# Moving the marks of two wide pairs from VectorE to GpSimd in a two-block sequence model

## What is computed

```python
dots = jnp.einsum('bhid,bhjd->bhij', q, k) * QK_SCALE
dots = jnp.einsum('hg,bgij->bhij', W_pre_th, dots)
dots = jnp.where(causal[None, None], mask_value, dots)
top = jax.lax.top_k(dots, TOPK)[0]
vk = top[..., -1:]
dots = jnp.where(dots < vk, mask_value, dots)
attn = jax.nn.softmax(dots, axis=-1)
attn = jnp.einsum('hg,bgij->bhij', W_post_th, attn)
```

## Time and profile before

| what | us |
|---|---|
| median of 3 runs | 3631.16 |
| profiled execution, its own time | 3634.36 |
| its span | 3633.1 |
| block 0 | about the first 850 |
| VectorE busy | 3437.1 |
| TensorE busy | 3390.1 |
| ScalarE busy | 3092.9 |
| GpSimd busy | 1745.4 |

### The profile page before, as it was taken

One profiled execution on the slowest core, in us unless ns is written; L12 is line 12 of the kernel. 1 busy time (PEld: TensorE's weight loads), 2 busy tenths in 40 slices (PEclk: granted clock), 3 DMA queues, 4 the chain that ended last, 5 costly groups with the idle time before them and its releaser, 6 DMA issues.

```text
span 3633.1 us, 78764 instructions
## 1 busy us (share of the span) xinstructions
PE 3390.1 (93%) x19287; PEld 2527.5 (70%) x19287; DVE 3437.1 (95%) x18664; ACT 3092.9 (85%) x10837; POOL 1745.4 (48%) x3670
## 2 busy tenths in 40 slices
PE   4999999986999999999999999999999999999987
PEld 2888888863666666676676666666666666666665
DVE  7999999936999999999999999999999999999993
ACT  6888888856898899989899898998998998898863
POOL 0000000014666666666666666666666666666663
PEclk9999999997999999999999999999999999999998
DMA  3000000002222222222222222222222222222210
GB/s 132 11 14 13 13 12 13 10 13 85 73 71 78 82 66 65 65 66 66 66 65 66 74 71 70 74 73 79 79 66 65 65 66 65 67 65 66 73 55 4
DMA packets 254141, 210.74 MB, mean 58 GB/s; under 512 B 78000, under 2 KB 234736, under 8 KB 252912
## 3 DMA queue, kind: packets, MB, share of 16 engines
q1 hardware_dynamic: 253680, 205.70, 18.1%
HBM read 93.97 MB, written 111.67 MB: 57 GB/s over the span
## 4 chain that ended last, share of the span: by engine, by line
PE 66%; ACT 17%; DVE 11%; issue 4%; POOL 2%; DMA 0%; SPq 0%; DVEq 0%; ACTq 0%; POOLq 0%
PE bank L378 10%; PE bank L221 8%; PE bank L1434 6%; PE bank L1422 5%; PE bank L1407 5%; PE bank L1465 3%; PE bank L469 3%; PE bank L195 3%; ACT SN L1618 3%; PE bank L1499 3%; DVE W L1826 3%; PE bank L1479 3%; PE bank L1438 3%; PE bank L346 3%; ACT sq L496 2%
## 5 line engine op out<-in xcount | busy, mean ns | idle before, releaser
L1826 DVE MATCH_REPLACE8 W<-last,W 128x130 f32<-128x130 f32 (+18 forms) x3456 | 871.9, 259 | 0.0
L1848 DVE MAX8 last<-W 128x8 f32<-128x130 f32 (+18 forms) x3456 | 762.9, 262 | 0.0
L1933 POOL TENSOR_SCALAR posts<-post,share 128x128 f32<-128x128 f32 x1024 | 366.7, 378 | 284.0 <-DVE share L1755 279.1
L1602 ACT ACTIVATE T<-T,peak 128x260 f32<-128x260 f32 (+15 forms) x1024 | 410.9, 409 | 3.5 <-POOL T L1984 2.4
L1618 ACT ACTIVATE SN<-bank,rq 128x260 f32<-128x260 f32 (+1 forms) x1024 | 357.9, 424 | 61.3 <-PE bank L1407 60.8
L1422 PE MATMUL bank<-T,pre 128*128 128x40 f32 (+15 forms) x1024 | 365.3, 439 | 14.4 <-ACT T L1626 10.1
L1434 PE MATMUL bank<-posts,T 128*128 128x128 f32 (+7 forms) x2048 | 311.7, 289 | 68.9 <-POOL posts L1933 60.6
L1984 POOL TENSOR_TENSOR T<-T,below 128x520 f32<-128x520 f32 (+12 forms) x416 | 360.3, 882 | 20.0 <-DVE below L1857 4.6
L1434 PEld LDWEIGHTS bank<-posts,T 128*128 128x128 f32 (+7 forms) x2048 | 249.0, 174 | 165.3 <-POOL posts L1933 88.9
L938 DVE TENSOR_TENSOR_SCAN hs<-dA,dx 128x256 f32<-128x256 f32 x512 | 349.9, 684 | 2.9 <-ACT dA L800 1.9
L1949 POOL TENSOR_TENSOR T<-T,w_mask 128x32 f32<-128x32 f32 x512 | 141.1, 278 | 412.6 <-ACT T L1626 410.2
(11 more groups left out here) (242 smaller groups left out, 9572.3 us busy)
## 6 DMA issues: line engine op xcount, KB each, us to landing
scores_by_token<-SN SPq DMA_DIRECT2D x64, 520.0 KB, 2.6
scores_by_token<-SN SPq DMA_DIRECT2D x64, 396.0 KB, 3.1
scores_by_token<-SN SPq DMA_DIRECT2D x32, 780.0 KB, 3.3
scores_by_token<-SN SPq DMA_DIRECT2D x32, 264.0 KB, 2.6
scores_by_token<-SN SPq DMA_DIRECT2D x32, 260.0 KB, 2.0
T<-scores_by_token SPq DMA_DIRECT2D x32, 244.0 KB, 3.0
T<-scores_by_token SPq DMA_DIRECT2D x32, 228.0 KB, 3.2
T<-scores_by_token SPq DMA_DIRECT2D x32, 212.0 KB, 3.8
```

The costliest lines, as they stand in the source:

```text
L1602: act.activation(one, one, ACT.Exp, bias=peak[k % 2][:, j:j + 1], accum_out=total[k % 4][:, j:j + 1]).then_inc(e_made, 1)
L1826: dve.match_replace(both[:, s, at:to], best[n], both[:, s, at:to], LOWEST).then_inc(ranked, 1)
L1848: dve.max(best[n], both[:, s, at:to]).then_inc(ranked, 1)
L1933: pool.tensor_scalar(posts[(4 * k + j) % NP][:], post[:], share[k % 2][:, j:j + 1], 1.0, ALU.mult, ALU.mult).then_inc(posts_made, 1)
```

## The change

One list is changed. `CUT[i]` names the pairs of quad i whose marks VectorE writes. Quads 2 and 6 are taken out of it, so three wide pairs are left, those of quads 0, 4 and 7, and GpSimd writes the marks of the other six.

```diff
     DROPS = [[j0 for j0 in (0, 2) if QUAD[i][j0 + 1] not in WHOLE] for i in range(QUADS)]
     DROPS_ALL = sum(len(c) for c in DROPS)
-    CUT = [[0], [], [0], [], [0], [], [0], [0]]
+    CUT = [[0], [], [], [], [0], [], [], [0]]
     CUT_ALL = sum(len(c) for c in CUT)
```

## The result

| what | before | after |
|---|---|---|
| median of 4 runs, us | 3631.51 (3630.14 to 3633.04) | 3748.99 (3745.88 to 3750.66) |
| ratio | | 1.0327, 95% interval 1.0314 to 1.034 |
| profiled execution, its own time | 3634.36 | 3745.88 |
| its span | 3633.1 | 3744.6 |

The table has a fourth run of before beside the three of the text ahead of the prediction, which moves its median from 3631.16 to 3631.51. The forecast was 3714 us with a range up to 3745. The sign, and both places where time is lost, came out as forecast; the size was 35 us too small, and the time lies just outside the range. Here is part 1 of the page of after, to be held against the earlier trace rows.

A forecast was written before the change was run, and what follows sets the result against it. VectorE, 95% busy, was taken to bound the kernel. Quad 2's part, 32 x 1.58, plus quad 6's, 31 x 1.03, made 82.5 us over the median of 3631.16: 3714 us, range 3655 to 3745.

The forecast's parts named there:

- What bounds, and the frame: VectorE, 95% busy, hardly waits and makes the 84.76 us period; time is counted by when it reaches each step.
- Quad 2's gain, capped at `x_c`: First norm's end: 0.63 us saved by quad 2's marks, only 0.18 usable before VectorE waits for TensorE's spread.
- The price of a mark of 228 columns: GpSimd's marks of quad 2: interpolated from neighbours near 1.05 us each, 2.28 us for two.
- Rival 4: GpSimd marks cost only double their VectorE time, 0.60 us at 228 columns: 3652 us, chance 2%.
- The wait that opens quad 4: VectorE's reduction opening quad 4 waits for GpSimd's add of quad 2, starting 1.76 us late each period.
- What hangs on that wait: Quad 2's part: the late quad 4 start is its whole price, net 1.58 us a period, 50.6 us in 32.
- The quad 6 mark: GpSimd's pair of 164-wide marks takes 2.50 us (1.86 to 2.82), making VectorE's `x_d` step 1.25 us late.
- The quad 6 sum: Second norm: 1.25 us late at `x_d` less 0.22 of today's wait, 1.03 us a period, 31.9 us in 31.
- two-strings case: Quad 4's opening and the second norm both bind: 3714 us, own range 3680 to 3748, chance 76%.
- Rival 1: The gain holds, as GpSimd's add and the second norm's root still arrive in time: 3608 to 3593 us, 6%.
- Rival 2: Only quad 4's start binds; GpSimd's delay after quad 6 is absorbed before the spread: 3664 us, 10%.
- rival 3: Only the second norm after quad 6 binds, net 0.85 us a period: 3658 us, chance 3%.

The follow-up runs named there:

- Quad 2 split and alone: Kernel before with only quad 2's marks on GpSimd, written ahead of quad 0's posts (beat 70), their add left at beat 73: 3623.93 us, ratio 0.9992.
- the split: Changed kernel with quad 2's marks written ahead of quad 0's posts (beat 70), their add left at beat 73: 3659.2 us, ratio 1.0087.
- the third buffer: Changed kernel with a third threshold buffer (`last8`), so a ranking waits for the drops of quad k - 3, not k - 2: 3661.32 us, ratio 1.0092.
- The cheap mark: Kernel before with only quad 6's marks on GpSimd, the two wide ones made as a plain product with zero: 3637.41 us, ratio 1.002.
- the place behind the hide: Quads 2 and 4 on GpSimd, marks apart from adds; marks now issued after the same beat's hide of masked keys: 3623.01 us, was 3740.68.

## Why the prediction was right and wrong, step by step

- **What bounds, and the frame.** Right. Time was to be counted in VectorE's frame, and 3.55 of the 3.57 us a period are found at eight places on VectorE, most of them waits or longer steps that the moved work explains.
- **Quad 2's gain, capped at `x_c`.** Right: 0.13 us usable where 0.18 was taken. Quad 2 split and alone gave 0.9992.
- **The price of a mark of 228 columns.** Right: an undisturbed one took 1.05 us, as interpolated. Rival 4 (cheap marks) is out.
- **The wait that opens quad 4.** Right in place, cause and size: 1.76 forecast, 1.72 found. Taken with what quad 2 gains it is 1.59 us against 1.58.
- **What hangs on that wait.** Wrong, and the largest part: the failed step. The prediction took that wait as the whole price of quad 2's part, 50.6 us: "Both ends hang on the reciprocal, an event of VectorE itself, so nothing catches up." That is true, and yet more is lost; lengthened steps of VectorE and the clock were put at nothing. Quad 2 alone cost 110 us, and taking quad 2 out of the change (by the split, or by the third buffer) gave back 88 to 90. Of these some 55 are the wait, 17 are rarer falls of the clock with the split, and about 10 are the step of quad 4 that the later add holds. The rule of the Trainium skill ("SBUF — State Buffer", Who interferes with whom) was weighed only for VectorE's steps that lengthen GpSimd's marks; the reverse, which of VectorE's steps the moved adds would meet, was never asked. All held steps of after together are 0.30 us at quad 4 and part of another 0.26.
- **The quad 6 mark.** Oversized. A pair took 2.13 us from start to start against the 2.50 that I chose. All four steps that I counted as disturbing fell beside the first mark, and together they made it only 0.29 us longer (1.122 us); the second ran undisturbed (0.834 us, as the interpolation has it). Counted from the maxima (2109.28 before, 2159.53 after), `x_d` came 0.83 us late in a usual period, not 1.25, and the root of the second norm 1.5 us later, not 1.81.
- **The quad 6 sum.** Its 32 us were measured as 31, but by two errors that cancel: `x_d` gave some 0.65 us, and 0.34 came from the share of quad 7, a wait that I had left outside the sum ("if that reaches VectorE later, up to 0.5 more", of TensorE's lateness). The cheap mark speaks against TensorE's lateness too, for the share still waits when `x_d` no longer does; before, that place has 0.03 us of slack. And in periods without a fall of the clock this part costs 42 us, which rarer falls bring down to 31. That the term was met is luck.
- **Clock.** Not foreseen at all. The 0.22 us of today's wait at `x_d` that I subtracted belongs to it: before, that step is some 1.0 us later in the 7 periods with a fall and hardly waits in the others. I asked nothing of what TensorE would do in its longer idle time. The waits at quad 6's share that go with the falls are 0.37 us a period, 12 us; against the falls of before, the net is 7 us.
- **The range.** My own bounds for the two-strings case went up to 3748, and I left the last of that out of the range. With holding and the clock outside the working, the upper bound was made of the same terms as the centre, only larger, and so was too low.
- **Rivals.** Rival 1 (a gain) is out for this change. Rival 2 (only quad 4) and rival 3 (only the norm) are out: quad 6 alone costs 31 us, and quad 2 costs 86 to 90 us on top.

What stays open: what decides in which periods the clock falls, whether VectorE or ScalarE makes the wait at quad 7's share, which GpSimd instructions hold a VectorE step, and which engine pays when the two start within some 0.05 us of each other.

## What to carry to other kernels

Work moved to a half-idle engine is paid where that engine's next instructions are due, so follow each of them in written order up to whoever waits, and then ask which two-input steps of VectorE its two-input adds will run into at their new time. If a moved instruction must wait, put it behind everything the waited-for engine needs in that stretch, and split it from what reads two inputs if a gap is free: the split was worth 89 us here, and the place behind the hide 118. When a change moves lateness about, carry on the sum past the wait you found, and take the upper bound from mechanisms that are not in the centre. When two variants are compared, set periods with and without a fall of TensorE's clock apart: here a kernel was 0.2% faster although its periods without a fall were as long as before.

## What the runs showed of the hardware

- **A GpSimd add holds a VectorE step with two SBUF inputs, a GpSimd mark does not.** 1.26 instead of 0.37 us beside the add of 456 columns that started 0.13 us earlier; 0.40 us for a wider step in the middle of two marks of 244 columns. It is the marks that get longer (1.122 against 0.834 us at 164 columns). A plain product of one tile with constants did hold a step, 0.43 instead of 0.31 us, so the number of tiles read isn't what tells them apart.
- **Either engine can pay.** Where two steps of VectorE followed each other, it was the add that grew, 1.15 to 1.41 us; with the starts in the same order and as close, VectorE's step grew from 0.30 to 0.99 us in another kernel.
- **Price by form on GpSimd.** Two instructions of 164 columns of the same opcode took 2.04 us as a comparison with a threshold of each row and a product (0.29 of it beside VectorE's steps), and 0.81 as a plain product with constants.
- **TensorE's clock can cost a third party.** At a granted clock of 0.57 in one stretch of 4 us, VectorE stood 0.88 us at a reciprocal a few us later, and the period was 89.8 instead of 88.1 us. With quad 2 alone such a stretch followed 2.03 us of idle time of TensorE in 19 of 30 periods, and VectorE lost 1.5 us in each, half of it in a step beside a GpSimd product that it otherwise misses.
